# Cross-attention of a decoder layer: undivided exps, sums from a ones column of V, division behind the values, and a new interleaving

## The reference, cut to what matters

```
Q = query @ Wq.T ; K = key @ Wk.T ; V = value @ Wv.T      # query: x after the first norm, key = value = context
scores = einsum('bqhd,bkhd->bhqk', Qh, Kh) / sqrt(8)        # 16 heads of 8 features
out = einsum('bhqk,bkhd->bqhd', softmax(scores), Vh)       # softmax over the 128 keys
x = layernorm(x + out.reshape(b, s, 128) @ Wo.T)
```

## Time and profile before

| | |
|---|---|
| median of 3 runs | 387.41 us (386.73 to 387.95) |
| the profiled execution: its time, its span | 386.72 us, 384.8 us |
| PE busy | 305.1 us, 79% of the span |
| DVE busy | 291.4 us, 76% |
| ACT busy | 268.4 us, 70% |
| POOL busy | 228.2 us, 59% |
| mean granted TensorE clock | 0.918 |

### The profile page before, as it was taken

One profiled execution on the slowest core, in us unless ns is written; L12 is line 12 of the kernel. 1 busy time (PEld: TensorE's weight loads), 2 busy tenths in 40 slices (PEclk: granted clock), 3 DMA queues, 4 the chain that ended last, 5 costly groups with the idle time before them and its releaser, 6 DMA issues.

```text
span 384.8 us, 5604 instructions
## 1 busy us (share of the span) xinstructions
PE 305.1 (79%) x1688; PEld 188.0 (49%) x1688; DVE 291.4 (76%) x462; ACT 268.4 (70%) x682; POOL 228.2 (59%) x148
## 2 busy tenths in 40 slices
PE   4999507999999998999999999788999764089700
PEld 3443305555566554554554558335666553079600
DVE  2849788999999999999999967697777636102335
ACT  3589766999999988999999964598999941022100
POOL 7500817999999988889888721154454534400063
PEclk9999855999999999999999999999999997559955
DMA  6986211133233332223330000000000000210212
GB/s 159 306 248 219 61 55 52 59 110 104 62 113 106 112 109 97 83 96 111 109 110 2 1 0 3 1 0 3 0 2 1 3 2 14 71 40 17 53 41 68
DMA packets 16770, 26.92 MB, mean 70 GB/s; under 512 B 1965, under 2 KB 10309, under 8 KB 16741
## 3 DMA queue, kind: packets, MB, share of 16 engines
q1 hardware_dynamic: 16036, 25.46, 21.2%
q0 software_dynamic: 704, 1.10, 1.0%
HBM read 24.00 MB, written 2.56 MB: 69 GB/s over the span
## 4 chain that ended last, share of the span: by engine, by line
PE 34%; DVE 31%; issue 10%; POOL 10%; ACT 9%; DMA 4%; SPq 0%; DVEq 0%; POOLq 0%; ACTq 0%
DVE arena L1127 20%; PE bank L687 12%; POOL arena L441 5%; PE bank L908 5%; DVE acc L1137 3%; PE bank L1002 3%; ACT arena L649 2%; PE bank L1010 2%; PE bank L825 2%; PE bank L981 2%; PE bank L747 2%; POOL dispatched_tokens L475 2%; PE bank L725 2%; POOL arena L481 2%; PE bank L927 2%
## 5 line engine op out<-in xcount | busy, mean ns | idle before, releaser
L441 POOL TENSOR_TENSOR arena<-arena,k_maskT 128x1024 f32<-128x1024 f32 x64 | 150.9, 2382 | 42.0 <-DVE arena L1114 21.5
L1127 DVE TENSOR_TENSOR_SCAN arena<-bank,arena 128x512 f32<-128x512 f32 x128 | 146.3, 1206 | 0.9 <-ACT bank L578 0.9
L687 PE MATMUL bank<-ident,arena 128*128 128x128 f32 (+1 forms) x686 | 102.2, 286 | 42.8 <-DVE arena L1127 23.5
L687 PEld LDWEIGHTS bank<-ident,arena 128*128 128x128 f32 (+1 forms) x686 | 77.2, 144 | 107.4 <-DVE arena L1127 69.9
L578 ACT ACTIVATE bank<-delta,a_neg 128x508 f32<-128x508 f32 x128 | 88.4, 692 | 10.1 <-DVE arena L1127 6.4
L825 PE MATMUL bank<-conv_in_T,ident 128*128 128x512 f32 x192 | 93.7, 598 | 0.0
L589 ACT ACTIVATE conv_in_T<-bank,c_col 128x256 f32<-128x256 f32 x192 | 80.3, 472 | 11.4 <-PE bank L687 10.6
L467 POOL TENSOR_TENSOR arena<-arena,rsum 128x1024 f32<-128x1024 f32 x16 | 30.4, 1897 | 36.9 <-DVE rsum L1219 36.9
L649 ACT ACTIVATE arena<-arena 128x128 f32<-128x128 f32 x128 | 37.7, 295 | 7.0 <-DVE arena L1214 6.8
L825 PEld LDWEIGHTS bank<-conv_in_T,ident 128*128 128x128 f32 x192 | 31.8, 192 | 15.8 <-issue 15.0
L1032 DVE COPY arena<-bank 128x160 f32<-128x160 f32 (+2 forms) x20 | 8.1, 433 | 33.3 <-PE bank L1010 17.6
(11 more groups left out here) (161 smaller groups left out, 343.3 us busy)
## 6 DMA issues: line engine op xcount, KB each, us to landing
k_maskT<-b_rows SPq DMA_DIRECT2D x32, 512.0 KB, 3.7
w_sb<-in_L_ffn_w SPq DMA_DIRECT2D x1, 2048.0 KB, 11.2
dispatched_tokens<-zeros SPq DMA_DIRECT2D x1, 640.0 KB, 16.4
expert_outputs<-arena SPq DMA_DIRECT2D x4, 160.0 KB, 2.1
x_tok<-in_x SPq DMA_DIRECT2D x1, 512.0 KB, 3.9
ctx_tok<-in_ctx SPq DMA_DIRECT2D x1, 512.0 KB, 4.1
out<-arena SPq DMA_DIRECT2D x2, 256.0 KB, 2.3
arena<-dispatched_tokens SPq DMA_DIRECT2D x1, 384.0 KB, 3.8
```

The lines of the kernel that those rows point to most:

```text
L441: gp.tensor_tensor(dBx[g % 2][h], du[:, dr, h, :], b_bc[:, g % RING, :], ALU.mult).then_inc(dBx_ok, 1)
L687: return pe.transpose(dst, src, ident[0:src.shape[0], 0:src.shape[0]])
L1127: ve.tensor_tensor_scan(o, a, v, 0.0, ALU.mult, ALU.add).then_inc(scanned, 1)
```

## The change

- The queries are no longer masked: `qT` is one plain copy per half. `scores` takes for group g only the 32 rows of its features, of the queries and of `k_maskT`.
- One exponential over all 128 x 1024 elements of a step stands in the place of eight with sums. `invert_sums` and POOL's multiplication are gone; `turn_probs` waits for the exponentials alone.
- The ninth column of each head's slot in `v_pad` is 1, so that the product with V holds the sum of the exponentials as a ninth value of each head (POOL fills the column in a second memset).
- New: `turn_values` transposes the four groups of a batch's values back (token by feature), `normalize_values` (DVE) inverts the 16 sums and multiplies, `turn_out` transposes the 128 x 128 result, ACT copies it (`oT`), and `project_out` is one product with Wo^T, which is turned together with Wq, Wk and Wv. The padded Wo, its memset and copy on POOL, its four transposes and its copy on ACT are gone.
- The order: probabilities and values are worked on one iteration earlier. On odd i PE runs turn_values ahead of turn_probs, on even i turn_out ahead of it and project_out behind weigh_values. DVE adds the residual ahead of the scores of odd i, divides behind them, and takes the moments in the iteration after. ROUTE0 is 2B+1; the counting and placing of the first half of the tokens are drawn into the loop, before the last residual.

```diff
-            gp.memset(v_pad[:, :, :, DH:32], 0.0).then_inc(v_zero, 1)
+            gp.memset(v_pad[:, :, :, DH + 1:32], 0.0).then_inc(v_zero, 1)
+            gp.memset(v_pad[:, :, :, DH:DH + 1], 1.0).then_inc(v_zero, 1)
             rstds(0)
-            for i in range(2 * B):
-
-                gp.wait_ge(sums_ok, i + 1)
-                gp.tensor_tensor(prob[i % 3], prob[i % 3], rsum[:, i % 3, :].unsqueeze(2).to_broadcast([P, CH, S]),
-                                 ALU.mult).then_inc(prob_ok, 1)
...
-            evacuate("qkv", qkvT[:, :, :], lambda ap: tiles(ap[:, 0:3 * D], 3))
-            evacuate("woT", woT[:, :, :], lambda ap: tiles(ap, HEADS // GH))
+            evacuate("qkv", qkvoT[:, :, :], lambda ap: tiles(ap, 4))
...
-            for g in range(2, HEADS // GH):
-                last = sc.activation(q_maskT[:, g, half(0)], src, ACT.Copy, scale=group_mask[:, g:g + 1])
-            was_read("q0", last)
+            evacuate("q0", qT[:, half(0)])
             evacuate("x1T1", x1T[:, half(1)])
...
-                    for h in range(CH):
-                        last = sc.activation(prob[i % 3][:, h, :], prob[i % 3][:, h, :], ACT.Exp, scale=SCALE,
-                                             accum_out=rsum[:, i % 3, h:h + 1])
-                    last.then_inc(exp_ok, 1)
-                if 2 <= i < 2 * B + 2:
-                    c = i - 2
+                    sc.activation(prob[i % 3], prob[i % 3], ACT.Exp, scale=SCALE).then_inc(exp_ok, 1)
+                if 1 <= i < 2 * B + 1:
+                    c = i - 1
...
-                if i % 2 == 0 and 4 <= i < 2 * B + 4:
+                if i % 2 == 1 and 3 <= i < 2 * B + 3:
+                    b = i // 2 - 1
+                    if b >= 2:
+                        to_read(sc, f"avq{b - 2}")
+                    evacuate(f"av{b}", avT[b % 2])
+                if i % 2 == 1 and 5 <= i < 2 * B + 5:
                     b = i // 2 - 2
                     if b >= 2:
                         to_read(sc, f"wo{b - 2}")
-                    evacuate(f"av{b}", outT[b % 2])
+                    evacuate(f"oT{b}", oT[b % 2], lambda ap: ap[:, 0:S])
...
                 for g in (2 * c, 2 * c + 1):
-                    last = pe.matmul(bank[:, g, :], q_maskT[:, g, S * b:S * b + S],
-                                     k_maskT[:, b, :, :].rearrange("p j k -> p (j k)"), start=True, stop=True)
+                    in_g = slice(GH * DH * g, GH * DH * g + GH * DH)
+                    last = pe.matmul(bank[:, g, :], qT[in_g, S * b:S * b + S],
+                                     k_maskT[in_g, b, :, :].rearrange("p j k -> p (j k)"), start=True, stop=True)
...
+            def turn_values(b):
+                wait_read(pe, f"av{b}")
+                dst = to_fill(pe, f"avq{b}")
+                for g in range(HEADS // GH):
+                    last = turn(dst[:, S * g:S * g + S], avT[b % 2][:, S * g:S * g + S])
+                filled(f"avq{b}", last)
+
+            def turn_out(b):
+                wait_read(pe, f"avq{b}")
+                dst = to_fill(pe, f"oT{b}")
+                filled(f"oT{b}", turn(dst[:, 0:S], o_tok[b % 2]))
+
+            def project_out(b):
+                wait_read(pe, f"oT{b}")
+                dst = to_fill(pe, f"wo{b}")
+                filled(f"wo{b}", pe.matmul(dst[:, 0:D], oT[b % 2], qkvoT[:, 3, :], start=True, stop=True))
...
             for i in range(LAST):
                 if 1 <= i < 2 * B - 1:
                     scores(i + 1)
+                if i % 2 == 1 and 5 <= i < 2 * B + 5:
+                    turn_values(i // 2 - 2)
+                if i % 2 == 0 and 6 <= i < 2 * B + 6:
+                    turn_out(i // 2 - 3)
+                if 1 <= i < 2 * B + 1:
+                    turn_probs(i - 1)
                 if 2 <= i < 2 * B + 2:
-                    turn_probs(i - 2)
-                if 3 <= i < 2 * B + 3:
-                    weigh_values(i - 3)
...
+                    weigh_values(i - 2)
+                if i % 2 == 0 and 6 <= i < 2 * B + 6:
+                    project_out(i // 2 - 3)
                 if i == ROUTE0:
                     gate_logits(0)
-
-            count_tokens(0)
+                if i == ROUTE0 + 2:
+                    count_tokens(0)
...
+            def normalize_values(b):
+
+                by_head = to_read(ve, f"avq{b}").rearrange("p (h e) -> p h e", h=HEADS)
+                link(ve.reciprocal(inv_sum[:, :], by_head[:, :, DH]))
+                if b >= 2:
+                    to_read(ve, f"oT{b - 2}")
+                was_read(f"avq{b}", ve.tensor_tensor(o_tok[b % 2].rearrange("p (h e) -> p h e", h=HEADS),
+                                                     by_head[:, :, 0:DH],
+                                                     inv_sum[:, :].unsqueeze(2).to_broadcast([P, HEADS, DH]), ALU.mult))
...
             for i in range(LAST + 1):
-                if i < 2 * B:
-                    shift_scores(i)
-                if 1 <= i <= 2 * B:
-                    invert_sums(i - 1)
-                if i == 3:
-                    was_read("q1", mask_queries(1, range(HEADS // GH)))
-                if i % 2 == 0 and 6 <= i < 2 * B + 6:
+                if i % 2 == 1 and 7 <= i < 2 * B + 7:
                     b = i // 2 - 3
                     src = to_read(ve, f"wo{b}")
                     was_read(f"wo{b}", ve.tensor_tensor(res2[:, b, :], src[:, 0:D], x1[:, b, :], ALU.add))
-                    wait_read(ve, f"wo{b}")
-                    moments_of(res2, b)
-                if i == 2 * B + 1:
+                if i < 2 * B:
+                    shift_scores(i)
+                if i == 3:
+                    evacuate("q1", qT[:, half(1)])
+                if i % 2 == 1 and 5 <= i < 2 * B + 5:
+                    normalize_values(i // 2 - 2)
+                if i % 2 == 0 and 8 <= i < 2 * B + 8:
+                    wait_read(ve, f"wo{i // 2 - 4}")
+                    moments_of(res2, i // 2 - 4)
+                if i == 2 * B:
                     normalize(res2, x2, 1, 0, x2_ok)
                 if i == ROUTE0:
                     evacuate("x2T0", x2T[:, half(0)])
-            choose_expert(0)
+                if i == ROUTE0 + 1:
+                    choose_expert(0)
+                if i == ROUTE0 + 3:
+                    place_tokens(0)
             normalize(res2, x2, 1, 1, x2_ok)
-            place_tokens(0)
```

More of the change, by code:

```diff
@@ L884, in queries @@
                 dst = to_fill(pe, f"q{g}")
[L885 removed]
+                filled(f"q{g}", pe.matmul(dst, qkvoT[:, 0, :], x1T[:, half(g)], start=True, stop=True))
             for g in range(2):
@@ L1193, in _ @@
             normalize(res1, x1, 0, 1, x1_ok)
-            def mask_queries(th, groups):
-                src = to_read(ve, f"q{th}")
-                for g in groups:
-                    last = ve.tensor_scalar(q_maskT[:, g, half(th)], src, group_mask[:, g:g + 1], None, ALU.mult)
-                return last
-            mask_queries(0, range(2)).then_inc(q_first_ok, 1)
             def shift_scores(i):
```

80 lines of the change are left out of this document (30 added, 50 removed).

## The result

The changed kernel takes 383.36 us (median; 382.21 to 384.22), the kernel before beside it 387.38: ratio 0.9892, interval 0.9863 to 0.9921. So it is faster, by 4 us (1.1%) and not by the 10 forecast.

The account below looks back on a forecast made before the run. PE bounded the loop at 7.62 us a batch; after, a ring of 6.85. Terms -0.4, -1.5, -3.0, -4.2, -0.8 sum to -9.9: profiled 386.72 becomes 376.8, median 377.5 us; 8-in-10 range 373 to 382.

Parts of the forecast that it names:

- Start of the program: Before the attention: Wo is turned with the other weights and the padded Wo's copy goes; -0.4 us.
- Start of the attention: Up to the first maximum: one plain query copy and 32-row products replace masks and full products; -1.5 us.
- The 0.43 more: Extra us for a pair of 32-row score products if strict program order limits overlap; the forecast did not add it.
- Steps 0 to 4: First attention steps: DVE alone limits at 2.48 us a step, and a query copy replaces 2.67 of masks; -3.0 us.
- Steps 4 to 15: Steady attention loop, 5.5 batches: 6.85 us a batch in place of 41.88 us in all; -4.2 us.
- the ring that was named: Loop: residual, maximum, subtraction, exponential, ACT's copy, transposes, values, projection, back to residual; 6.85 us per two steps.
- rival 1: Loop: PE stays the bound, through poor overlap or shape changes costing 0.76 on both sides; 385.3 or 383.3 us, chance 0.09.
- case for full rows: Rival 1's first case, in the loop: 32-row products don't overlap as hoped; 7.8 to 7.9 us per batch, 385.3 us.
- From step 15 on: Last maximum through last projection to last scatter: 13.3 us to the projection's end, then scatters less delayed; -0.8 us.
- term of 6.2 us to the last values: Tail, last maximum to last values: the sum of 2.48, 1.06, 0.97, 1.00 and 0.65.
- Rival 3: Attention loop: TensorE's clock falls because PE idles; slower, about 405 us if all batches run at 1.2 GHz; chance 0.04.
- if the clock row falls before the routing: Sign on record, in the trace after: a clock falling ahead of the routing would show the prediction wrong.

Follow-up runs that it names:

- f1: Kernel before the change, with seven unread 128-column products on TensorE ahead of its wait for x: 386.12 us, ratio 0.9971.
- e6: Changed kernel with seven unread 128-column products on TensorE ahead of its wait for x, none in the tail: 378.76 us, ratio 0.9781.
- e3: Changed kernel with each step's exponentials as eight instructions of 128 columns: 384.21 us in one execution, 7.56 us per batch for 6.92.
- e4: Changed kernel with ACT's copy of the transposed probabilities cut into two halves of one bank each: 377.38 us, 6.50 us per batch for 6.92.
- e8: Changed kernel with the residual of odd steps behind DVE's maximum and subtraction: 378.54 us in one execution, 6.81 us per batch for 6.92.
- e2b: Changed kernel with scores over all 128 rows again and no group masking, so another output: 388.41 us in one execution, 7.49 us per batch.
- e1: Changed kernel run again with nothing edited: 382.3 us, ratio 0.9838, tail 34.7 us.
- e5: Changed kernel with unread 256-column products in PE's waits in the last batches, ahead of the second half's gate logits and within both: 377.99 us.
- f2: Changed kernel with unread products at the start and in the tail's waits, and ACT's copy of the probabilities in two halves: 374.7 us, ratio 0.9671.
- e9: Changed kernel with only those of e5's unread products that stand in iterations 16 to 20: 379.57 us, ratio 0.9806.

## Why the prediction was wrong

**Start of the program, -0.4: right** (1.17 for 1.57). But the sum took the start of one profiled execution as given. Over all runs whose start was not touched the row copy lay between 22.30 and 24.88 us; the profile of before had 22.48. This is chance and not the change: 2.4 us in the profiled execution, and f1 makes it about 1.3 in the median of the kernel before. So a part of the miss isn't in any step of the sum: with the start set early (e6) the median is 378.76, 1.3 above the forecast, in a run whose clock also held late in the tail.

**Start of the attention, -1.5: right**, and so was its basis. From L505 to the first maximum it is 221.53 us (26.05 to 247.58) for 223.19 (24.05 to 247.24), -1.7. The pair of scores takes 1.13 where 1.14 was forecast. The page "TensorE: Matmul & The Clock Gate" of the Trainium skill (Part 3, The mechanism) states that matmuls start and end strictly in program order, and also that tiles in different row groups overlap. The 0.43 more was my reading of the first for products of two instructions each; with this reading the trace disagrees (1.13 for the four instructions).

**Steps 0 to 4, -3.0:** measured -3.4. The first two maxima are 2.40 apart, where DVE's pitch was forecast as 2.48.

**Steps 4 to 15, -4.2:** measured -3.9, a period of 6.92 for 6.85, and by the ring that was named: DVE waits at the residual, 0.95, and PE, ACT and DVE are all idle in between. Experiments e3 (+0.64), e4 (-0.43) and e8 (the next ring) each moved it as its links say. Single terms were off and nearly cancelled: from the transposes to the residual it is 2.09 for 1.92 (the projection alone 0.49 for 0.40), from the exponentials to ACT's copy 0.96 for 1.06. The 0.76 us without a load stand only on the way out of a pair of scores; on the way in there are 0.20 or none. The drain at each change of tiling mode, which the page "TensorEngine Tiling (Array Packing)" of the Trainium skill (Key Properties) states, agrees with the trace on the one side and doesn't show at such a price on the other, so rival 1 stayed away. Its case for full rows was too dear as well: e2b gives 7.49 where 7.8 was worked out.

**From step 15 on, -0.8: this is the step that failed.** It measured +2.8 in the first profile and +5.3 in e1. What lies behind the last projection was right: the fifth scatter waits for slots, `place_tokens(0)` delays the last residual by 0.7 (projection done at 312.75, residual at 313.47), and to the last scatter it is 15.3. The path to the end of the last projection, 13.3 in the sum, took 17.0, for two reasons.

The first is its term of 6.2 us to the last values (6.6 with its hand-overs). It left out what the ring of the loop had: the last transposes wait for ACT's copy of the step before (1.21 ahead of 300.38), and ahead of the last values PE has the values of the step before, a projection, the residual's wait and the turned values of a batch. Where the clock stayed full that long, the last values ended 8.37 us (e5, 301.69) and 8.36 us (e6) behind the last maximum: 1.8 more than forecast. In e4b, where that copy is in two halves, it is 7.92.

The second is the clock. I took every PE duration of the last batches at 2.4 GHz, as the earlier trace rows had them, for a path on which PE waits for ACT and DVE over and over: 0.80 and 1.21 ahead of the last transposes, then 0.48, 0.88, 0.52. From the last maximum to the end of the last projection PE was busy for 11.2 of 17.0 us at a mean clock of 0.83; filled up in e5, for 13.0 of 15.1 at full clock (293.32 to 308.40). The last values ended 9.8 us behind the last maximum, 1.4 more than at full clock, and from there to the end of the last projection it is 7.2 us for e5's 6.7, which is what was forecast. That is 1.9 of the 3.7 us, and the rows agree: 1.94 for 1.06, 1.08 for 0.65, 0.77 for 0.46, with 0.2 in two smaller ones. The second half's gate logits, 1.85 for 1.03, are no part of it, since they took 1.84 before. In e1, where the clock didn't come back between as it did here at 303.5, the path took 19.5 us. Filled waits (e5) bring the tail to 29.6 and f2's to 29.0, not to the forecast's 28.6: the 1.8 of the first reason stay, and the second half, at full clock only in runs with these products, gives back some 0.8.

Why the clock falls in this stretch isn't shown. The waits alone don't tell before from after: in the same stretch of before (302.67 to 316.20) PE was busy for 9.3 of 13.5 us and the clock stayed full, with a wait longer than any of those after:

```profile
304.79 1.07 PE L687 MATMUL bank<-ident,arena 128*128 128x128 f32 x8 [1.63 <-ACT arena L660]
```

Nor does what stood ahead of it, a PE busy for all of 30.47 us, where after it was 25.6 of 27.7: in e2b PE was busy for 29.73 of 29.97 us of the loop, and the clock fell 6.0 us behind the last maximum all the same. The clock row of e2b's page, down from slice 31 on (9.7 us each):

```profile
PEclk9999855999999999999999999999999855559955
```

Rival 3 had the mechanism and not the place. I asked whether the clock falls in the loop, where PE waits some tenths at a time (it never did), and for the tail allowed "1 us either way" for the point where the clock rises again. The point where it falls was not in the sum. The sign I put on record, "if the clock row falls before the routing", is what happened.

**Open:** what makes the clock rise early or late in executions of the same code; why it falls 4 us behind the last maximum in some profiles and 14 in others, with nothing added to the tail, and 19 in the kernel before; whether the products in iterations 16 to 20 hold it or e9's execution was one of the late ones; and whether the loop's waits count, which were not filled in any run.

## What to carry to other kernels

When a change takes work off TensorE, read at each later stretch how long it will wait between its pieces, and price the pieces there at both levels of the clock: here a stretch that TensorE had passed at full clock lost 1.9 us to it in one execution and more in the next. Walk the ring of the loop through the last steps as well: links that stand ahead of every step stand ahead of the last one too, and leaving them out cost the forecast 1.8 us. Before costing against one profiled execution, look at whether its start and its clock are typical; and find a loop's ring by name, since cutting one link (a copy in two halves) gave 0.43 us a batch for more work.

## What the hardware showed that was not expected

- Unread products make a kernel faster: with 32 matmul instructions more in the tail (153 for 121) it takes 29.6 us, in the profiles without them 30.9 to 34.7.
- With nothing added there, TensorE's clock fell 4.3 us behind the last maximum in the first profile and 13.9 in e6; a loop in which PE is never idle (e2b) didn't keep it up.
- TensorE's clock at the start differs between executions of the same code: L707 took 3.41, 2.35 and 1.73 us, and seven products ahead of the data set it to 1.73.
- Two 32-row fp32 score products of 512 columns in different row groups take 1.13 us, over all rows up to 1.98.
- One exponential of 1024 columns takes 1.06 us, eight of 128 columns 1.70; the copy out of PSUM 1.01 in one, 1.07 in two.
